# A recurrent layer's TensorE program as one counted loop over pairs of steps with branches, and two empty steps before the second feed-forward product

## What is computed

```python
def step(carry, x_t):
    h_prev, c_prev = carry
    combined = jnp.concatenate((x_t, h_prev), axis=1)
    f_t = jax.nn.sigmoid(combined @ W_f + b_f)
    i_t = jax.nn.sigmoid(combined @ W_i + b_i)
    c_tilde = jnp.tanh(combined @ W_c + b_c)
    c_t = f_t * c_prev + i_t * c_tilde
    o_t = jax.nn.sigmoid(combined @ W_o + b_o)
    h_t = o_t * jnp.tanh(c_t)
    return ((h_t, c_t), h_t)
```

## Time and profile before

| | us |
|---|---|
| median of 3 runs (6681.10 to 6689.14) | 6681.84 |
| time of the profiled execution | 6686.47 |
| its span | 6684.7 |
| first step's first matmul | 1395.2 |
| chunks 1 to 4, 256 steps each | 888.3, 892.4, 887.4, 889.4 |

### The profile page before, as it was taken

How to read it: one execution, slowest core, us unless ns; L and a number is a source line. 1 busy time by engine, 2 the same in 40 slices (tenths; PEclk the granted TensorE clock), 3 DMA queues, 4 the chain that set the end, 5 groups by cost and what they waited for, 6 DMA issues and landing times. The chain is left out here.

```text
span 6684.7 us, 407138 instructions
## 1 busy us (share of the span) xinstructions
PE 5272.5 (79%) x179105; PEld 3612.1 (54%) x179105; DVE 3797.7 (57%) x22378; ACT 1842.5 (28%) x8915; POOL 681.9 (10%) x716
## 2 busy tenths in 40 slices
PE   1567967788877788777897778887777777887999
PEld 1233324466655566555666556665555555554545
DVE  7305776656666666666666666666666666565111
ACT  1111007623333333333333333333333333200100
POOL 0722426400000000000000000000000000252000
PEclk7789988899999999999999999999999999998999
DMA  2114537501000000000010000100000000222100
GB/s 95 51 33 102 136 96 211 153 12 29 21 0 0 8 27 26 0 0 0 24 29 7 0 0 12 29 18 0 0 0 0 0 0 0 71 77 60 67 32 16
DMA packets 172013, 241.52 MB, mean 36 GB/s; under 512 B 90361, under 2 KB 130937, under 8 KB 167826
## 3 DMA queue, kind: packets, MB, share of 16 engines
q0 software_dynamic: 41952, 116.33, 6.3%
q1 hardware_dynamic: 129714, 120.73, 5.9%
HBM read 224.38 MB, written 12.61 MB: 35 GB/s over the span
## 5 line engine op out<-in xcount | busy, mean ns | idle before, releaser
L1654 PE MATMUL l_bank<-l_w,l_hp 128*32 128x128 f16 x160000 | 2488.2, 220 | 827.2 <-DVE l_hp L1942 799.8
L1654 PEld LDWEIGHTS l_bank<-l_w,l_hp 128*32 128x32 f16 x160000 | 2255.6, 97 | 1435.9 <-DVE l_hp L1942 1390.6
L1906 DVE STREAM_TRANSPOSE agg<-l_bank 128x128 f32<-128x128 f32 x2500 | 792.5, 317 | 1177.9 <-PE l_bank L1654 1007.5
L1782 ACT ACTIVATE l_th<-l_z 128x8 f32<-128x8 f32 x2500 | 523.7, 209 | 2153.8 <-DVE l_z L1912 2153.8
L1664 PE MATMUL l_spare<-l_w 128*2 128x512 f16 x12120 | 866.1, 379 | 4.8 <-issue 4.7
L2128 POOL DMA_INDIRECT ga_rows<-r_table,dst_t x176 | 167.2, 950 | 4638.9 <-DMA r_table<-c_r 4511.5
L1787 ACT ACTIVATE l_tc<-l_th 128x2 f32<-128x2 f32 x2500 | 490.7, 196 | 466.2 <-DVE l_th L1929 466.2
L1918 DVE SCALAR_TENSOR_TENSOR l_terms<-l_th 128x4 f32<-128x4 f32 x2500 | 357.5, 143 | 256.4 <-ACT l_th L1782 256.4
L1936 DVE TENSOR_TENSOR l_hp<-l_go,l_tc 128x2 f16<-128x2 f32 x2500 | 421.8, 169 | 131.7 <-ACT l_tc L1787 0.9
L1912 DVE TENSOR_REDUCE l_z<-agg 128x8 f32<-128x24 f32 x2500 | 447.4, 179 | 42.5
L1942 DVE TENSOR_TENSOR l_hp<-l_full,l_hp 128x2 f16<-128x2 f32 x2500 | 422.3, 169 | 43.7 <-DVE l_full L1937 0.4
(11 more groups left out here) (425 smaller groups left out, 4892.4 us busy)
## 6 DMA issues: line engine op xcount, KB each, us to landing
w<-in_g_W SPq DMA_DIRECT2D x128, 128.0 KB, 2.1
w<-in_l_Wx SPq DMA_DIRECT2D x128, 128.0 KB, 2.1
keys<-in_src_by_tile SPq DMA_DIRECT2D x7, 1344.0 KB, 6.4
e_w<-in_e_W SPq DMA_DIRECT2D x2, 4096.0 KB
e_chosen<-chosen SPq DMA_DIRECT2D x24, 256.0 KB, 6.0
wh<-in_l_Wh SPq DMA_DIRECT2D x1, 4096.0 KB, 19.1
late<-in_l_Wh SPq DMA_DIRECT2D x1, 4096.0 KB
late<-in_l_Wx SPq DMA_DIRECT2D x1, 4096.0 KB
```

The source lines that it names most:

```text
L1654: mm = pe.matmul(banks[par][q][32 * j:32 * j + 32, 0:128], hp[:, par, k, 30 - 30 * v:62 - 30 * v], w16[:, half, k, j, 256 * q + 128 * v:25 ...
L1782: act.activation(th[:, 2 * q:2 * q + 2, 1:], z[:, q, :].rearrange("p (j m) -> p j m", m=GATES), ACT.Tanh, scale=2.0 ** -Z_BITS).then_inc(s ...
L1906: dve.transpose(turn[:, par, q, :, 1:33], banks[par][q][:, 0:128].rearrange("p (m r) -> p m r", r=32)).then_inc(s_turned[q], 1)
```

## The change

TensorE's program for a chunk becomes one loop of 128 pairs of steps. After a step's 128 matmuls, now always without filler of their own (`bare=True`), a tree of comparisons with the loop's counter u (a pair, so slice 2u + p) picks the piece that follows: a turned block, a unit, a norm's matmuls, or plain filler. A unit now comes behind two groups of filler (`fill((1, 2))`) where it had one. The pieces of all stages stand in the loop's body, once for each parity. The waits of a unit count from the chunk's start (`at`), for which the counts of `piece_in` start at 16 * `M16`; nothing else about the loads changes.

The second part: a slice number `HID_IN` = 42 is put in and `FF2` begins at 44, so slices 42 and 43 have no TensorE work; VectorE's last product of FF1 stays at 42. Everything from FF2 on moves by two slices; the plain steps are 152 instead of 154. VectorE's and ScalarE's written-out parts grow by two steps a chunk and are otherwise the same.

```diff
-TURN, WO, LNF, FF1, FF2, LNL, XIN, STEPS = 0, 4, 12, 26, 42, 58, 70, 102
+TURN, WO, LNF, FF1, HID_IN, FF2, LNL, XIN, STEPS = 0, 4, 12, 26, 42, 44, 60, 72, 104
...
-            def step(t, par, busy=False, bare=False):
+            def step(t, par, bare=False):
...
-                for k in range(0 if bare else 1 if busy else 3):
+                for k in range(0 if bare else 3):
                     unread(k)
...
-                with pe.Fori(start, end, 1) as u:
-                    for p in range(2):
-                        step(u * 2 + (a + p), p, busy=True)
-                        unit(c, stage, u, p, src)
...
+            def below(u, value, then, other):
+                with pe.If_lt(pe.to_reg(u), value):
+                    then()
+                with pe.Else():
+                    other()
...
+                def units(u, p, stage, second=False):
+                    first = stage + 2 * KC * second
+                    fill((1, 2))
+                    if stage == FF2 and p == 0:
+                        wait_dve(pe, c, HID_IN if second else FF1 + 8)
+                    unit(c, stage, u, p, source(c, stage, second), at=stage // 2)
+
+                def norm(u, p, stage):
+                    j = (0, 4) if p == 0 else (1, 3)
+                    plain = lambda: fill(range(3))
+                    only(u, (stage + j[0]) // 2, lambda: norm_step(c, stage + j[0]),
+                         lambda: only(u, (stage + j[1]) // 2, lambda: norm_step(c, stage + j[1]), plain))
+
+                def piece_of(u, p):
+                    early = lambda: below(
+                        u, LNF // 2,
+                        lambda: below(u, WO // 2,
+                                      lambda: below(u, 1, lambda: turn_block(c, p), lambda: turn_block(c, 2 + p)),
+                                      lambda: units(u, p, WO)),
+                        lambda: norm(u, p, LNF))
+                    middle = lambda: below(
+                        u, HID_IN // 2, lambda: units(u, p, FF1),
+                        lambda: below(u, FF2 // 2, lambda: fill(range(3)),
+                                      lambda: below(u, FF2 // 2 + KC, lambda: units(u, p, FF2),
+                                                    lambda: units(u, p, FF2, True))))
+                    last = lambda: below(u, XIN // 2, lambda: norm(u, p, LNL),
+                                         lambda: below(u, STEPS // 2, lambda: units(u, p, XIN), lambda: fill(range(3))))
+                    below(u, FF1 // 2, early, lambda: below(u, LNL // 2, middle, last))
+
+                with pe.Fori(0, W // 2, 1) as u:
                     for p in range(2):
-                        step(u * 2 + (a + p), p, busy=True)
-                        unit(c, stage, u, p, src)
...
+                        step(u * 2 + (a + p), p, bare=True)
+                        piece_of(u, p)
...
             for c in range(1, CHUNKS):
...
                 pe.wait_ge(s_divided, 2 * c + 2)
                 wait_act(pe, c - 1, STEPS - 1)
-                for i in range(WO):
-                    step(a + i, i % 2, bare=True)
-                    turn_block(c, i)
-                steps_with_units(c, WO, 0, KC)
-                steps_with_norm(c, LNF)
-                steps_with_units(c, FF1, 0, 2 * KC)
...
-                with pe.Fori(a + STEPS, a + W - 2, 2) as t:
-                    step(t, 0)
-                    step(t + 1, 1)
...
+                chunk(c)
```

More of the change, by code:

```diff
@@ L1547, in _ @@
         def _(sp):
+            for p in range(2):
+                sp.sem_inc(piece_in[p], 16 * M16)
             wait_pe(sp, 0, LNF - 1)
@@ L1641, in first_rows @@
                         if stage == FF2 and u % KC == 0:
-                            wait_dve(pe, 0, FF2 if u else FF1 + 8)
+                            wait_dve(pe, 0, HID_IN if u else FF1 + 8)
                         for p in range(2):
@@ L1689, in steps_with_norm @@
-            def steps_with_norm(c, stage):
-                a = (c - 1) * W
-                end = FF1 if stage == LNF else XIN
-                plain = stage + 5 + (stage + 5) % 2
-                for i in range(stage, plain):
-                    step(a + i, i % 2, bare=on_pe(i))
-                    if on_pe(i):
-                        norm_step(c, i)
-                with pe.Fori(a + plain, a + end, 2) as t:
-                    step(t, 0)
-                    step(t + 1, 1)
+            def below(u, value, then, other):
[3 more added lines that the diff above has]
+                    other()
@@ L1873, in rows_step @@
                                           gate[:, 0:1, :].broadcast_to([P, 2, W]), ALU.mult).then_inc(row_dve, 1)
-                elif i <= FF2 and i % 2 == 0:
+                elif i <= HID_IN and i % 2 == 0:
                     m = (i - FF1) // 2 - 1
```

43 lines of the change are left out of this document (19 added, 24 removed).

## The result

| | before | after |
|---|---|---|
| median of the runs on one chip | 6681.47 us (6673.62 to 6689.14) | 6820.07 us (6811.14 to 6823.48) |
| time of the profiled execution | 6686.47 | 6821.53 |
| its span | 6684.7 | 6819.7 |
| first step's first matmul | 1395.2 | 1397.0 |
| four chunks | 3557.5 | 3693.2 |

The ratio is 1.0204, with a 95% interval of 1.0192 to 1.0216: the change makes the kernel 139 us **slower**. The span grew by 135.0 us, and the four chunks alone by 135.7.

A forecast was written before the change was run, and what follows sets the result against it. No engine is full; a chain through h bounds each step at 3.413 us. From 6684.7, less 15.6 net gain, plus 175 (unit steps), 6 (plain) and 8 (second norm): 6858 span, 6855 us median, range 6640 to 6940.

The forecast's parts named there:

- The bound and the floor: No engine is full; a chain through h sets each step's floor, 3.413 us, 3494.9 us for the four chunks' 1,024 steps.
- The plain steps: Steps with only filler: comparisons delay it 0.88 us, nearly hidden before h; 0.01 us taken in 152 steps a chunk, 6 us.
- What the change removes: In the four chunks, the wait at slice 42 with slow loads after it (13 us) and straight-code holes; at most 62.6 us.
- The first pairs: At each chunk's start, two steps that fetch the new loop body: up to 15.7 us, taken as 11, 44 in all.
- The steps with units: 288 steps grow by their comparison chain's length minus 0.21 us: 43.8 us a chunk, 175 in four.
- lead of the sequencer: TensorE's sequencer is about 12 pairs ahead, so the comparisons begin 0.19 us before a step's last weight load.
- the room: TensorE's spare time in a plain step before h is there: 0.79 us plus some 0.07.
- The second norm: Its steps meet one comparison more, chain up to 1.21 us: about 0.2 us in ten steps a chunk, 8 us.
- other leftovers: In the four chunks, what stays of ScalarE's and VectorE's own holes: 3 us.
- Rival 1: Comparisons ahead of filler and unit are hidden, the sequencer getting further ahead: 6637 to 6667, say 6655 us; chance 0.16.
- Rival 2: The loop body doesn't stay on the chip and is fetched again each pair: 8.2 or 14.7 ms; chance 0.10.
- Rival 3: Jumps inside the loop body cost only what falling through does, 0.13 us each: 6770 us; chance 0.18.

## Why the prediction was right, and where its steps were off

The forecast was 6855 us and a range of 6640 to 6940, and 6820 was measured: slower by 139 us instead of 173. The range was 300 us wide, so a hit on it says little; the periods and the sums by stage say more. The mechanism was the forecast's, and the order of the comparisons, changed alone, showed it. Point by point:

**The bound and the floor** held. The plain steps stayed at 3.41 us, and all of the growth lies in the four chunks. h comes 3.19 us after a step's start in both kinds of step that are shown.

**What the change removes** held: slices 42 and 43 at the floor, LNF down by 13.6 us, LNL by 8.6, 70 packets where about 72 were forecast.

**The first pairs** were oversized: 29.3 us over the floor, 7.3 a chunk, against 11. The lower end of the forecast, 6, was nearer. The forecast priced the whole body at the straight code's pace. What the trace shows is a few long holes, most of them at jumps (1.5, 3.4 and 2.5 us in chunk 1), and a term that the forecast didn't have: about a third of the 29.3 us, 10.5, is the lower clock behind the holes. So the nearness of the sum is in part luck. Of the code of later stages, which is read when they come, almost nothing shows; which part is read when was not told apart.

**The steps with units**: forecast 43.8 us a chunk over the floor, measured 164.2/4 = 41.1. In this sum four terms are off, in both directions. All times count from the start of the step's last weight load, in us:

| | forecast | measured |
|---|---|---|
| lead of the sequencer | 0.19 | 0.152 |
| a comparison taken, passed | 0.27, 0.13 | 0.26, 0.128 |
| XIN: filler starts | 0.75 | 0.757 |
| FF2, first half: filler starts | 0.74 | 0.884 |
| from two filler groups to the unit | 0.38 + 0.215 | 0.541 |
| from the unit to the next step | 1.29 - 0.24 | 1.061 |
| growth: XIN | 0.73 | 0.645 |
| growth: FF2, first and second half | 0.72, 0.86 | 0.77, 0.90 |
| growth: WO and FF1 | 0.32 | 0.25 |

- The lead was a little smaller, 0.15: the comparison starts while the last 11 or so weight loads are still to come.
- The second filler group was priced right (0.217 by the run with one group), but the first was priced with what had stood behind it before (0.38 from filler to unit in the earlier trace rows); behind the chain one group takes 0.32. That is 0.05 of the 0.08 by which XIN was too dear; 0.04 is that the filler had already stood that far behind the last load's start before (1656.28 in the earlier trace rows, the last load's start being at 1656.24), which the forecast took as zero.
- FF2 was miscounted. Its first half takes three comparisons and passes two, not two and three: the third, which asks for slice 42, is left by a jump too. The sequencer's row shows it, with a median of 202 ns among five. That is 0.13 more in each of these steps, and one more jump than counted in the second half.
- WO and FF1 gained from both smaller terms, and had the smallest chain.

**The plain steps** were forecast at +6 us with up to 90 in the range. They cost nothing. The step that failed is the room: it was read from the matmuls' idle time (0.79), and these ends are modelled; by the run with four comparisons the filler needs 0.65 and not 0.82. The error cost little here because both answers lay near zero, but it decided the expectation for one more comparison, which missed by 69 us.

**The second norm** was forecast at +8 us and stands 4.2 over the floor. Its steps with a fifth comparison are late, but not as the forecast had it. Half of the loss, 2.2 us, is in slices 63 and 64, whose norm matmuls come behind the five comparisons (3.73 to 3.78 and 3.64 us a step). The rest is mostly in odd steps with filler (3.48 to 3.52 us), and there the sequencer itself is what ends last: at slice 65 of chunk 1 h is written by 1650.95, the loop's last register instruction starts at 1650.97, and the next step's weights follow at 1651.06. The forecast had put the jump and the loop's end at nothing; here they cost up to 0.1 us a step.

Summed: first pairs 44 to 29.3, the units' steps 175 to 164.2, plain steps 6 to 0, the norm 8 to 4.2, other leftovers 3 to about 1. That is 236 us over the floor forecast, against 198.8 measured: every one of these sums was too high, none was made good by another.

**The rivals** fell. Rival 1 (the decisions are hidden) needs h to stay the releaser in XIN with 0.3 us or more of idle; the row there is 0.33 and names nobody, and the filler starts 0.66 us after the loads. The milder form that was tested, that only the second filler group costs something, is refuted by the run with one group, which is still 1.3% slower than before. Rival 2 (the loop doesn't stay on the chip) needs hundreds of packets; there are 70. The Trainium skill's warning in "Runtime: NRT & Kernel Launch", Instruction fetch mechanics, of two resident blocks of 16 KB, finds no support in this case: a body of 1,162 instructions, five or six such blocks, ran 512 times out of 70 packets for the whole program. The store of 128 KB that the same section gives would explain it; no run here had a body larger than that. Rival 3 (cheap jumps inside the body) needs 0.13 us for a jump; the rows have 202 ns and 0.26 to the next.

By the 0.11 us for a compare-and-branch that the Trainium skill states ("Advanced Engine Details and Errata", Control Flow Timing), one figure for taken and passed, the units' steps would have come to about 60 us over the floor, an estimate. They stand 164 over it, so the rows of this trace were the better price: one taken comparison costs more than twice the page's figure, and one passed slightly more.

## What to carry to other kernels

Before a branch is put into a loop whose steps wait for one another, count the comparisons on the way to each piece, price them as taken or passed, and set that against the time until the data that the step waits for is there; a decision is free in front of idle time and paid in full in front of work that already fills the step. Ask for the commonest tight piece first, and put work that every piece has ahead of the comparisons. Small loops, one for each stage, had the advantage of both sides here: little code to wait for in the norms, and no decision ahead of a unit.

## What the runs showed of the hardware that was not expected

- Register instructions that prepare a wait take about 0.1 us each from start to start (recorded as 36 ns). They cost 0.1 to 0.2 us in each XIN step as soon as no filler stood in front of the unit.
- The recorded end of a train of matmuls is later than the time at which the next train can start: 12 filler matmuls are recorded with 0.82 us, and with four comparisons more the next step's first matmul started 0.65 us after the filler's first load.
- A hole that goes with straight code is 0.33 to 0.44 us in the norm steps shown, but up to 3.4 us at the first jumps of a loop's body.
- Holes of 1.5 us and more cost twice: the granted clock was 0.50 to 0.64 over the matmuls of the steps behind them, until the fourth step of a chunk.
- Open: the XIN steps of chunk 3 are 23.3 us over the floor against 20.8 in the other three chunks. The longer ones are odd steps (4.22 instead of 4.06 us), and the 0.16 us lies inside the filler: its eight weight loads start within 0.20 us instead of 0.03. The loop without the empty steps has it too in chunk 3 (23.4 against 20.8), and so has the other order of the comparisons (15.5 against 12.4); with one or four more comparisons in the plain steps it is gone (20.9), though the XIN pieces are the same. Each chunk has its own copy of the body, so where the piece stands in the program seems to matter. No experiment was made on it.
